# Reading the expert gates into all partitions as two transfers of 64 partitions instead of one of 128

## The reference, cut to what matters

```python
x = x + conv(ln_c(x), ...)                # windowed attention, 32 windows of 64 tokens
t = to_tokens(x)
xt = ln_t(t).reshape(N, D)                # N = 2048 tokens, D = 64
logits = xt @ Wr + br                     # 8 experts
probs = softmax(logits)
top_p, top_idx = top_k(probs, 2)
weights = top_p / top_p.sum(-1)
xn = layernorm(xt)
h = gelu(einsum('end,edh->enh', xn * ln_g[e] + ln_b[e], W1) + b1)     # 8 experts, 256 hidden
y = einsum('enh,ehd->end', h, W2) + b2
out = sum over the 2 chosen experts of weights * y
x = t + out
```

## Time and profile before

| | us |
|---|---|
| median of 3 runs | 213.57 (213.45 to 214.53) |
| the profiled execution | 212.58 |
| its span, first to last instruction | 210.9 |
| TensorE busy | 164.8 (78%), mean granted clock 0.921 |
| VectorE busy | 118.8 (56%) |
| ScalarE busy | 101.6 (48%) |
| GpSimd busy | 49.6 (24%) |
| bytes moved by transfers | 17.05 MB |

### The profile page before, as it was taken

How to read it: one execution, slowest core, us unless ns; L and a number is a source line. 1 busy time by engine, 2 the same in 40 slices (tenths; PEclk the granted TensorE clock), 3 DMA queues, 4 the chain that set the end, 5 groups by cost and what they waited for, 6 DMA issues and landing times.

```text
span 210.9 us, 4268 instructions
## 1 busy us (share of the span) xinstructions
PE 164.8 (78%) x1584; PEld 98.2 (47%) x1584; DVE 118.8 (56%) x340; ACT 101.6 (48%) x201; POOL 49.6 (24%) x94
## 2 busy tenths in 40 slices
PE   7979899998899796981499963988969297993622
PEld 7856323358776565660055630546434253550111
DVE  3675778868824859778801589514953249302223
ACT  0556767774439866543066422554545055462000
POOL 6818453007531132713400024000410000000000
PEclk9999999999969999999569999999999879999555
DMA  6987995970000000000001110011210111111110
GB/s 156 216 217 194 306 317 166 413 307 2 3 0 3 3 3 0 3 5 0 3 34 49 47 52 21 20 45 52 74 44 37 47 71 49 35 47 50 71 48 25
DMA packets 11299, 17.05 MB, mean 81 GB/s; under 512 B 1992, under 2 KB 7760, under 8 KB 11152
## 3 DMA queue, kind: packets, MB, share of 16 engines
q1 hardware_dynamic: 10672, 16.51, 23.9%
q10 hardware_dynamic: 608, 0.28, 0.5%
HBM read 12.00 MB, written 4.78 MB: 80 GB/s over the span
## 4 chain that ended last, share of the span: by engine, by line
DMA 32%; DVE 26%; PE 26%; issue 7%; SPq 6%; ACT 2%; POOL 0%; POOLq 0%; DVEq 0%
DMA GB<-gates 22%; DMA SCN<-moved 5%; DMA gates<-GT 3%; PE PS L514 3%; DVE SCN L1105 3%; PE PS L675 3%; PE PS L611 3%; SPq L354 2%; DVE GM L1153 2%; PE PS L558 2%; SPq L336 2%; DMA moved<-TMG 2%; SPq L341 1%; PE PS L686 1%; DVE ON L1190 1%
## 5 line engine op out<-in xcount | busy, mean ns | idle before, releaser
L955 ACT ACTIVATE HR<-PS,B1P 128x512 f32<-128x512 f32 x64 | 39.4, 690 | 26.5 <-PE PS L698 26.5
L709 PE MATMUL PS<-HR,W2s 128*64 128x512 f32 x128 | 32.8, 636 | 4.0 <-DVE GM L1153 3.4
L697 PE MATMUL PS<-X,W1H 128*128 128x512 f32 x64 | 28.4, 443 | 0.0
L698 PE MATMUL PS<-X,W1L 128*128 128x512 f32 x64 | 26.7, 418 | 0.0
L1153 DVE SCALAR_TENSOR_TENSOR GM<-PS,B,GB 128x512 f32<-128x512 f32 x12 | 9.0, 749 | 18.8 <-DMA GB<-gates 18.8
L1153 DVE SCALAR_TENSOR_TENSOR AC<-PS,B,GB 128x512 f32<-128x512 f32 x4 | 3.0, 751 | 26.7 <-DMA GB<-gates 21.0
L709 PEld LDWEIGHTS PS<-HR,W2s 128*64 128x64 f32 x128 | 8.1, 143 | 20.4 <-issue 14.8
L932 ACT ACTIVATE BV<-PS 64x256 f32<-64x256 f32 x32 | 12.3, 383 | 7.9 <-PE PS L595 7.5
L1172 DVE TENSOR_TENSOR SR<-PS,SCN 128x512 f32<-128x512 f32 x16 | 10.5, 684 | 9.0 <-PE PS L611 8.6
L697 PEld LDWEIGHTS PS<-X,W1H 128*128 128x128 f32 x64 | 13.2, 206 | 5.0 <-issue 2.5
L698 PEld LDWEIGHTS PS<-X,W1L 128*128 128x128 f32 x64 | 13.2, 206 | 2.4
(11 more groups left out here) (142 smaller groups left out, 295.6 us busy)
## 6 DMA issues: line engine op xcount, KB each, us to landing
moved<-TMG SPq DMA_DIRECT2D x16, 256.0 KB, 3.1
SCN<-moved SPq DMA_DIRECT2D x8, 512.0 KB, 6.9
GB<-gates SPq DMA_DIRECT2D x16, 256.0 KB
W1R<-in_W SPq DMA_DIRECT2D x2, 512.0 KB, 7.1
W1E<-in_W SPq DMA_DIRECT2D x2, 256.0 KB, 5.5
W2s<-in_W SPq DMA_DIRECT2D x1, 512.0 KB, 4.7
out<-XR SPq DMA_DIRECT2D x4, 128.0 KB, 14.6
REL<-in_rel SPq DMA_DIRECT2D x2, 225.0 KB, 5.2
```

What stands on the lines that cost most here:

```text
L697: nc.tensor.matmul(ps[:, :], W1H[:, col:col + P], X2[:, j * 512:j * 512 + 512], start=True, stop=False)
L698: end(nc.tensor.matmul(ps[:, :], W1L[:, col:col + P], X2[:, j * 512:j * 512 + 512], start=False, stop=True), "h", n)
L709: m = nc.tensor.matmul(ps[d * C:d * C + C, :], W2s[:, 2 * (2 * ep + d) + c, :], HR[(4 * u + 2 * c + d) % 8][:, :], start=(c == 0), stop=(c ...
L955: A(HR[n % 8][:, :], PS[b][:, :], ACT.Gelu, bias=B1P[:, col:col + 1]).then_inc(bank_drained[b], 1)
```

## The change

Each of the four reads of `gates[j]` becomes two: one for each d, which repeats the one row `gates[j, ep, d]` over 64 partitions. Both raise `gates_in[ep]` by 16, so what waits on it waits for twice the count. Bytes, sources and destinations stay.

```diff
                 for ep in range(4):
                     if j:
-                        sp.wait_ge(gates_in[ep], 16 * j)
-                    sp.dma_start(GB[:, j % 2, ep, :],
-                                 gates[j, ep].unsqueeze(1).to_broadcast([2, C, 512])).then_inc(gates_in[ep], 16)
+                        sp.wait_ge(gates_in[ep], 32 * j)
+                    for d in range(2):
+                        sp.dma_start(GB[C * d:C * d + C, j % 2, ep, :],
+                                     gates[j, ep, d].partition_broadcast(C)).then_inc(gates_in[ep], 16)
...
-                    dve.wait_ge(gates_in[ep], 16 * (j + 1))
+                    dve.wait_ge(gates_in[ep], 32 * (j + 1))
```

## The result

| | us |
|---|---|
| median of 4 runs with the change | 192.36 (190.09 to 193.58) |
| median of 4 runs before, beside them | 213.73 (213.45 to 214.53) |
| ratio | 0.893, interval 0.885 to 0.901 |
| forecast | 193.1, range 191.0 to 198.0, a ratio of 0.904 |
| two more sets of 6 runs with the change | 192.72 and 192.89, ratios 0.907 (0.901 to 0.913) and 0.908 (0.903 to 0.913) |

The kernel is faster by some 21 us, and by the mechanism forecast; the first ratio, though, is slightly better than the range allows. Over all 16 runs the median is 192.7.

What follows compares the result with a forecast made beforehand. The prediction took the reads of gates into GB, on two of sixteen DMA engines, as the bound. Seven gains in TensorE's order sum to 20.5 us, taking the 213.57 us median to 193.1 us, range 191.0 to 198.0.

Steps and rivals of the forecast that it cites:

- The bound: Reads of gates into GB: two of 16 engines full at 49 GB/s, fourteen idle; VectorE waits 39.8 us.
- The second rule of the Trainium skill: Reads of gates: engines are the largest number up to 16 dividing both sides' slowest dimension; 2 before, 16 engines after.
- The rule against it: Reads of gates: transfers to disjoint partition halves share the same 16 engines and serialize, so the gain would be nil.
- Steps 2 to 7: TensorE, from the x2(2) transposes to the last output transposes: gains 1.57, 3.88, 1.58, 3.98, 7.94 and 0.45 us in turn.
- One sign: VectorE in the new profile: the first gate of a group should no longer wait over 4 us.
- Step 1: Gate of u = 1, on which TensorE's logits wait: its 1.08 us wait for GB goes, gain 1.08 us.
- The low end: Whole kernel: 192.1 us, the profiled execution less the sum, less 1.1 us of run spread, gives 191.0 us.
- Twice the present rate would do: Reads of gates: the end stays hidden down to 2.4 us per pair, 108 GB/s, and x2(3) then loses 0.2 us.
- nothing spreads: Rival on the reads of gates: the pair still runs at 49 GB/s and every wait stays, 213.6 us; chance 0.06.
- slower: Rival on the reads of gates: each half falls to one engine, a pair takes 10.7 us, some 284 us; chance 0.03.
- the source row is the limit: Rival on the reads of gates: sixteen engines on one repeated row get 75 GB/s, 3.5 us a pair, 199 us; chance 0.08.

Runs made afterwards that it cites:

- half_2x32: The changed kernel with each half's source walked as 2 x 32 x 512, 2 outermost instead of 64: 220.54 us, ratio 1.034 to the kernel before.
- cols: The changed kernel with each pair's two transfers divided by columns, 256 each to all 128 partitions, 2 outermost: 223.35 us, ratio 1.053 to the kernel before.
- noread: The changed kernel reading only the first group's gates, 24 of 32 transfers left out: 192.96 us beside 192.72 of the changed kernel.
- again: The changed kernel without an edit, for more runs and a second trace: 192.72 us (191.74 to 193.59).
- half_8x8: The changed kernel with each half's source walked as 8 x 8 x 512, 8 outermost instead of 64: 192.52 us, ratio 0.903.
- half_4x16: The changed kernel with each half's source walked as 4 x 16 x 512, 4 outermost instead of 64: 196.94 us.
- warm: The changed kernel with 28, 12, 6 and 6 unused identity products on TensorE before its waits for the router's gates: 189.54 us, ratio 0.886.
- third: The changed kernel without an edit a third time, as yardstick for the kernels with added identity products: 192.89 us (191.48 to 193.51).
- warm_again: The changed kernel with added identity products before the router's gates, run again beside the changed kernel on the same chip: 188.78 us (187.93 to 189.77).

## Why the prediction was right, and where it was not

- **The bound** (two engines full, fourteen idle): right. The engines follow the outermost count: the rates with 2 and 4 outermost (49 and 98 GB/s) and the shares of 0.26, 0.51 and 1.03 with 4, 8 and 16 show it; the division into halves is only a way to raise it. The second rule of the Trainium skill that the prediction named, from the page "DMA: Bandwidth & Descriptors", section "Why a DMA increments its semaphore by 16 and not by 1", is what these runs show: two engines for 2, four for 4, eight for 8, sixteen for 16. One reading in it was loose: a store of the result was issued at 191.34 us and so was also under way from 192 to 194 us; from 189 to 191 us, ahead of it, the share is 0.13 at 49 GB/s as well.
- **The rule against it**, from the same page of the Trainium skill, section "Rules for kernel authors", that two halves are not worth it: with the outermost count kept, half_2x32, which divides into such halves, agrees with its outcome (1.034), and so does cols, which divides by columns (1.053). Its reason does not hold here, since two engines work on these reads and not sixteen. It does not reach a division that also changes that count.
- **Steps 2 to 7** came out as worked, to within 0.3 us each: about half of VectorE's waits for GB turned into time; of the rest, 9.1 us stayed, off the path, and 8.9 became waits for TensorE's down product. noread shows no gain left in the reads of the groups 1 to 3. An issue took 0.60 us instead of 0.54, without effect. One sign failed: the first gate of a group still waited up to 5.6 us for GB in again, behind the late fourth store.
- **Step 1** was short by 0.69 us. The down product of u = 0 came 4.56 us after the first store instead of 5.16, because the clock rose earlier; from 109 to 111 us it is 1.00 in again and 0.88 before. So 0.60 of the excess stands there before any gate is used and is not the change's. What decides when the clock rises stays open; the sum took the clock of one trace as given.
- **The low end** is the step that failed: "less the 1.1 us by which the runs spread (213.45 to 214.53)". Measured, the spread is 3.5 us for the changed kernel (16 runs, 190.09 to 193.59) and 5.6 us for the kernel before (33 runs beside the later sets, 210.55 to 216.11); three runs were too few to know it. The two runs on which the ratio rests, 190.09 and 191.75 us, have mean clocks of 0.973 and 0.960, the other two 0.952; they were not traced. I counted a fall of the clock as a loss only, although the trace of before had its own low stretch near 106 us that could shorten. The term of the sum that was mis-sized is step 1, 1.08 where the trace shows 1.77.
- **"Twice the present rate would do"** was wrong: 98 GB/s cost some 4 us. The working beside it asked for 108 GB/s. The overhead before the first pair was taken from undivided reads at two engines (2.2); with two transfers per pair and four engines it was 3.3, and the store of gates can take 3.4 us to the first read behind it, where the sum had 1.7 for its landing.
- **The rivals**: "nothing spreads" and "slower" fell with the share of 0.49, "the source row is the limit" with half_8x8 (146 GB/s where it had supposed 75).

## What to carry to other kernels

When a transfer is slow, compare its DMA share with 1/16: 0.13 meant two engines, and the cause was the outermost count of the source, not its bytes or its partitions. Raise that count (by dividing, or by another order of the dimensions) before moving or overlapping the transfer. And count a wait only as far as the next engine in line is not itself late: 39.8 us of waits held 21 us of time.

## What was not expected of the hardware

- A store of 16 KB of gates, from its issue to the first read behind it, took 1.4 us in most groups, 2.0 to 2.4 in some, and 3.4 to 3.8 us in the third or fourth group of six traces (half_4x16: 173.08 to 176.46; warm: 151.38 to 154.97). No run tells why.
- The store of 128 KB of the result, issued behind the reads of GB on the same queue, landed the later the fewer engines worked on these reads: in a median of 14.6 us before and 12.0 and 9.0 in half_2x32 and cols, 6.8 in half_4x16, 3.2 in half_8x8, 2.2 in the changed kernel. No engine waited for it here.
- Two engines on halves of one repeated row were slower to begin than on two rows (half_2x32 against the kernel before: the first gate 9.1 instead of 7.5 us after the first issue, at the same 5.35 us per pair later).
- Products that add nothing shortened the kernel by 4.1 us. By the traces of third and warm_again some 3.3 of it stand where TensorE came to the next work at a granted clock of 1.00 (2.4 GHz) instead of one that had fallen to 0.50 (1.2 GHz).
